# Weight rounding and absolute sums on ScalarE, the feed-forward norms' last operation on GpSimd, and new hand-written orders

## What is computed

```python
x = layernorm(x + attn(x))          # 16 heads of 64, 4 key/value heads, rotary, ALiBi, softmax
x = layernorm(x + xattn(x, ctx))    # 16 heads of 16, windows of 64 and the one before, cell mask, 4 inner norms
x = layernorm(x + ffn(x))           # silu(bitlinear(x, w_gate)) * bitlinear(x, w_up), then w_down
# bitlinear: activations to int8 by row maximum, weights to -1, 0, 1 by the mean of their absolute values
```

## Time and profile before

| | |
|---|---|
| median of 3 runs | 2292.14 us |
| profiled execution | 2293.73 us, of which the span of the instructions is 2291.6 us |
| mean granted TensorE clock | 0.979 |
| PE busy | 2147.3 us (94%) |
| DVE busy | 1954.5 us (85%) |
| ACT busy | 1695.3 us (74%) |
| POOL busy | 1434.2 us (63%) |

### The profile page before, as it was taken

One profiled execution on the slowest core, in us unless ns is written; L12 is line 12 of the kernel. 1 busy time (PEld: TensorE's weight loads), 2 busy tenths in 40 slices (PEclk: granted clock), 3 DMA queues, 4 the chain that ended last, 5 costly groups with the idle time before them and its releaser, 6 DMA issues. The chain is left out here.

```text
span 2291.6 us, 57972 instructions
## 1 busy us (share of the span) xinstructions
PE 2147.3 (94%) x19370; PEld 1649.6 (72%) x19370; DVE 1954.5 (85%) x7981; ACT 1695.3 (74%) x4738; POOL 1434.2 (63%) x1678
## 2 busy tenths in 40 slices
PE   4799999999999999999999999999999999999964
PEld 3577777777777777777777777777777777777742
DVE  5678888889888889988888988888898888889874
ACT  1477777877787887778788777878877778877742
POOL 2466566667766667766666776666677666667531
PEclk8799999999999999999999999999999999999996
DMA  4111100111110001111001111100111110011100
GB/s 133 37 31 27 37 26 23 27 34 36 36 36 24 25 27 33 36 36 36 23 25 28 34 36 36 36 20 23 33 34 36 37 36 14 26 35 35 31 15 10
DMA packets 85397, 74.64 MB, mean 33 GB/s; under 512 B 18544, under 2 KB 79344, under 8 KB 85104
## 3 DMA queue, kind: packets, MB, share of 16 engines
q1 hardware_dynamic: 85104, 70.93, 11.1%
HBM read 45.72 MB, written 8.39 MB: 24 GB/s over the span
## 5 line engine op out<-in xcount | busy, mean ns | idle before, releaser
L1379 POOL TENSOR_TENSOR prob<-prob,precs 128x512 f32<-128x512 f32 x512 | 525.9, 1044 | 218.7 <-DVE precs L1014 216.0
L1287 ACT ACTIVATE prob<-prob,nmax 128x256 f32<-128x256 f32 x1024 | 509.3, 503 | 155.2 <-DVE nmax L1007 155.2
L1007 DVE CUSTOM_DVE_ANT_0 prob<-bank,alibi 128x256 f32<-128x256 f32 x1024 | 371.4, 419 | 13.5 <-PE bank L715 12.4
L611 PE MATMUL bank<-ident,prob 128*128 128x128 f32 x2048 | 315.9, 277 | 5.7 <-ACT pT L1294 5.0
L1311 ACT ACTIVATE px<-px,nmx 128x128 f32<-128x128 f32 x1024 | 315.1, 409 | 4.8 <-DVE nmx L1116 4.8
L1294 ACT COPY pT<-bank 128x512 f32<-128x512 f32 x512 | 300.3, 587 | 12.1 <-PE bank L611 12.0
L611 PEld LDWEIGHTS bank<-ident,prob 128*128 128x128 f32 x2048 | 236.7, 141 | 80.9 <-issue 43.3
L734 PE MATMUL bank<-pT,v_sb 128*64 128x256 f32 x2048 | 250.5, 386 | 5.9 <-DVE qq_lo L998 5.9
L1116 DVE CUSTOM_DVE_ANT_0 px<-bank,mask 128x128 f32<-128x128 f32 x1024 | 225.5, 285 | 29.1 <-PE bank L794 26.2
L623 PE MATMUL bank<-w_hi,x_hi 128*128 128x512 f32 (+1 forms) x512 | 199.2, 389 | 23.6 <-POOL x_lo L1359 16.6
L734 PEld LDWEIGHTS bank<-pT,v_sb 128*64 128x64 f32 x2048 | 142.7, 137 | 101.0 <-issue 45.6
(11 more groups left out here) (211 smaller groups left out, 6104.2 us busy)
## 6 DMA issues: line engine op xcount, KB each, us to landing
raw<-in_xT SPq DMA_DIRECT2D x32, 256.0 KB, 2.9
kx_tok<-in_ctx SPq DMA_DIRECT2D x32, 256.0 KB, 2.9
raw<-in_ctxT SPq DMA_DIRECT2D x32, 256.0 KB, 3.0
xtok<-in_x SPq DMA_DIRECT2D x32, 256.0 KB, 3.0
vs<-vx SPq DMA_DIRECT2D x64, 128.0 KB, 2.9
kx<-k_sin SPq DMA_DIRECT2D x256, 32.0 KB, 2.0
out_y<-x SPq DMA_DIRECT2D x32, 256.0 KB, 2.2
cellk<-in_cell SPq DMA_DIRECT2D x32, 64.0 KB, 3.4
```

What stands on the lines that cost most here:

```text
L611: last = nc.tensor.transpose(bank[:, n * P:(n + 1) * P], src, ident[:])
L1007: v.tensor_tensor_reduce(out=prob[:, (2 * p + q) % SLOTS, c, :], in0=psum[SCORES[c]][:, q * L:(q + 1) * L], in1=alibi[:, p % 2, :], scale= ...
L1287: nc.scalar.activation(prob[:, (2 * p + q) % SLOTS, c, :], prob[:, (2 * p + q) % SLOTS, c, :], ACT.Exp, bias=nmax[:, i:i + 1], scale=-1.0, ...
L1379: g.tensor_tensor(prob[:, n % SLOTS, :, :], prob[:, n % SLOTS, :, :], precs[:, 2 * n:2 * n + 2].unsqueeze(2).to_broadcast([P, 2, L]), ALU. ...
```

## The change

1. High parts of the weights: the copies of `first`, `prep 4` and `wo_split` are taken from DVE and given to ACT. DVE keeps the subtractions and waits for ACT by new semaphores (w_rounded, crossed_rounded).
2. Absolute sums: three DVE reductions become three ACT operations (Abs with an accumulator) that write their unused result over kx. They wait until wo, which lies in kx at first, has been split; kx_clear on POOL now waits for them.
3. SP: of the loads of group 0 only the bias rows still wait for the split of wqkv; wqx, wkvx, wox, ropex and pen go at once. ctx of batch 0 is loaded later, xtok and alibi earlier.
4. X2 and `out` go from ACT to POOL, as (y2 - mean) * rstd with two per-row operands; f_bias and z_bias are gone.
5. BODY, HEAD and TAIL of all five engines are new. On PE both BODYs hold the same 78 matmul steps.

```diff
@@ act
+                    if kind == "first":
+                        i, = args
+                        cols = slice(512 * i, 512 * i + 512)
+                        act.wait_ge(first_loaded[i], 16 * KT)
+                        for k in range(KT):
+                            nc.scalar.copy(w_hi[:, k, cols], raw_w[k][:, cols]).then_inc(w_rounded, 1)
+                    elif kind == "wo_split":
+                        act.wait_ge(later_loaded[1], 16)
+                        nc.scalar.copy(wo_hi[:], raw_wo).then_inc(wo_split, 1)
...
+                        if args[0] == 4:
+                            act.wait_ge(pre_dve, P_CENTRED)
+                            for hi, rawer in ((wkvx_hi, raw_kvx), (wqx_hi, raw_qx), (wox_hi, raw_ox)):
+                                nc.scalar.copy(hi[:], rawer).then_inc(crossed_rounded, 1)
+                        elif args[0] == 5:
+
+                            act.wait_ge(later_loaded[2], 16 * len(later_loads[2]))
+                            act.wait_ge(wo_split, 2)
+                            for m in range(3):
+                                if m > 0:
+                                    act.wait_ge(w_sums, m)
+                                nc.scalar.activation(kx[:].rearrange("p k h n -> p (k h n)"), stage[m], ACT.Abs, accum_out=wsum[:, m:m + 1])\
+                                    .then_inc(w_sums, 1)
...
-                    elif kind == "X2":
-                        act.wait_ge(*landed("stored", b - 1))
-                        act.wait_ge(*at("f_bias", b))
-                        for t in range(TT):
-                            ins = nc.scalar.activation(x2[:, t, :], y2[:, t, :], ACT.Identity, bias=f_bias[:, t:t + 1], scale=f_rstd[:, t:t + 1])
-                        ins.then_inc(sem["x2_ready"], 1)
...
@@ pool
+                    elif kind == "X2":
+                        pool.wait_ge(*landed("stored", b - 1))
                         pool.wait_ge(*at("f_neg", b))
                         pool.wait_ge(*at("f_rstd", b))
-                        g.tensor_tensor(f_bias[:], f_neg[:], f_rstd[:, 0:TT], ALU.mult).then_inc(sem["f_bias"], 1)
+                        pool.sem_inc(waits_passed, 1)
+                        for t in range(TT):
+                            ins = g.tensor_scalar(x2[:, t, :], y2[:, t, :], f_neg[:, t:t + 1], f_rstd[:, t:t + 1], ALU.add, ALU.mult)
+                        ins.then_inc(sem["x2_ready"], 1)
...
@@ BODY["pe"], cut
-        (4, 'HT', 0), (3, 'TX', 1, 1), (3, 'SX', 3), (2, 'T', 13), (3, 'OX', 0), (3, 'TX', 2, 0), (1, 'kT'),
-        (3, 'TX', 2, 1), (4, 'D', 0), (2, 'T', 14), (4, 'HT', 1), (3, 'TX', 3, 0), (1, 'qT', 1), (4, 'D', 1),
...
+        (4, 'HT', 1), (1, 'S', 0), (1, 'qT', 1), (3, 'TX', 3, 0), (4, 'D', 1), (3, 'TX', 3, 1), (2, 'T', 15), (1, 'S', 1),
+        (3, 'OX', 1), (1, 'Q', 0, 2), (3, 'BX', 0), (2, 'O', 3), (1, 'T', 0), (3, 'BX', 1), (1, 'Q', 1, 2), (3, 'NO'),
+        (1, 'T', 1), (1, 'S', 2), (1, 'T', 2), (3, 'PO'), (2, 'W', 1), (2, 'KV', 0), (1, 'V'), (1, 'qT', 2), (1, 'T', 3),
+        (1, 'S', 3), (2, 'KV', 1), (1, 'O', 0), (1, 'T', 4), (2, 'NX'), (0, 'K'), (3, 'XQ'), (1, 'T', 5), (1, 'S', 4),
...
+        (1, 'O', 2), (2, 'TX', 1, 0), (1, 'T', 12), (3, 'HT', 0), (2, 'TX', 1, 1), (2, 'SX', 3), (2, 'OX', 0),
+        (2, 'TX', 2, 0), (1, 'T', 13), (0, 'kT'), (3, 'D', 0), (2, 'TX', 2, 1), (1, 'T', 14),
@@ BODY["pool"], the places of the new steps
+        (2, 'R', 11), (2, 'R', 12), (4, 'HS', 1), (2, 'R', 13), (2, 'R', 14), (2, 'R', 15), (1, 'R', 0), (4, 'ZS'),
+        (1, 'R', 1), (4, 'out'), (1, 'R', 2), (2, 'C'), (1, 'Q', 0, 2), (3, 'OS'), (2, 'CS'), (1, 'Q', 1, 2), (3, 'FS'),
+        (1, 'R', 3), (3, 'X2'), (1, 'R', 4), (3, 'QN'), (1, 'R', 5), (0, 'X'), (1, 'R', 6), (2, 'KV', 1), (1, 'R', 7),
@@ HEAD["pe"], start
-        (0, 'first', 0), (0, 'first', 1), (0, 'V'), (0, 'K'), (0, 'Q', 0, 1), (0, 'Q', 1, 1), (0, 'first', 2),
-        (0, 'prep', 1), (0, 'prep', 2), (0, 'prep', 3), (0, 'qT', 0), (0, 'qT', 1), (0, 'Q', 0, 2), (0, 'Q', 1, 2),
-        (0, 'kT'), (1, 'K'), (0, 'prep', 5), (0, 'KV', 0), (0, 'S', 0), (0, 'S', 1), (0, 'qT', 2), (0, 'T', 0),
...
```

More of the change, by code:

```diff
@@ L115 @@
     "sp": [
-        (0, 'first', 0), (0, 'first', 1), (0, 'first', 2), (0, 'load_xT'), (0, 'tables', 0), (0, 'load_ctx'),
-        (0, 'loads', 0), (0, 'loads', 1), (0, 'load_cell'), (0, 'loads', 2), (1, 'load_xT'), (0, 'load_ctxT'),
-        (2, 'load_xT'), (0, 'load_xtok'), (0, 'tables', 1), (1, 'load_ctxT'), (1, 'load_xtok'), (1, 'load_ctx'),
-        (0, 'load_vs'), (0, 'kx_clear'), (0, 'fill_kx'), (1, 'load_cell'), (3, 'load_xT'), (2, 'load_ctx'),
-        (2, 'load_ctxT'), (2, 'load_xtok'), (2, 'load_cell'), (1, 'fill_kx'), (1, 'load_vs'), (0, 'store'),
-        (3, 'load_cell'), (4, 'load_xT'), (3, 'load_ctx'), (2, 'load_vs'), (2, 'fill_kx'),
+        (0, 'first', 0), (0, 'first', 1), (0, 'first', 2), (0, 'load_xT'), (0, 'tables', 0), (0, 'loads', 0),
+        (0, 'loads', 1), (0, 'load_cell'), (0, 'load_xtok'), (0, 'tables', 1), (0, 'loads', 2), (0, 'load_ctx'),
+        (1, 'load_xT'), (0, 'load_ctxT'), (2, 'load_xT'), (1, 'load_ctxT'), (0, 'kx_clear'), (0, 'fill_kx'),
+        (1, 'load_ctx'), (1, 'load_xtok'), (0, 'load_vs'), (1, 'load_cell'), (2, 'load_cell'), (3, 'load_xT'),
+        (2, 'load_xtok'), (2, 'load_ctxT'), (1, 'load_vs'), (2, 'load_ctx'), (1, 'fill_kx'), (0, 'store'), (4, 'load_xT'),
     ],
     "pe": [
[32 rows of a table removed]
+        (0, 'first', 0), (0, 'first', 1), (0, 'K'), (0, 'Q', 0, 1), (0, 'first', 2), (0, 'prep', 1), (0, 'prep', 2),
[33 rows of a table added]
     ],
@@ L158 @@
         (0, 'first', 0), (0, 'first', 1), (0, 'first', 2), (0, 'prep', 0), (0, 'tables', 0), (0, 'K'), (0, 'Q', 0, 1),
-        (0, 'Q', 1, 1), (0, 'prep', 1), (0, 'prep', 2), (0, 'prep', 3), (0, 'prep', 4), (0, 'qT', 0), (0, 'wo_split'),
[28 rows of a table removed]
+        (0, 'prep', 1), (0, 'prep', 2), (0, 'prep', 3), (0, 'Q', 1, 1), (0, 'prep', 4), (0, 'tables', 1), (0, 'qT', 0),
[30 rows of a table added]
     ],
     "act": [
[26 rows of a table removed]
+        (0, 'first', 0), (0, 'first', 1), (0, 'first', 2), (0, 'X'), (0, 'tables', 0), (0, 'Q', 0, 1), (0, 'Q', 1, 1),
[27 rows of a table added]
     ],
     "pool": [
[15 rows of a table removed]
[15 rows of a table added]
     ],
@@ L555, in run @@
                             sp.dma_start(gb[:].rearrange("p c k -> p (c k)"), a["gb"]).then_inc(gb_loaded, 16)
-                            sp.wait_ge(w_split, 12)
                         elif g == 2:
                             sp.wait_ge(pre_dve, P_CROSSED)
-                        for dst, src in later_loads[g]:
+                        for i, (dst, src) in enumerate(later_loads[g]):
+                            if g == 0 and i == 5:
+                                sp.wait_ge(w_split, 3 * KT)
                             sp.dma_start(dst, src).then_inc(later_loaded[g], 16)
@@ L914, in prepare @@
                         v.tensor_copy(turned_bias[:, m, :, :], psum[5 + m][:].rearrange("p (k n) -> p k n", k=KT)).then_inc(pre_dve, 1)
[L915 to L917 removed]
+                    dve.wait_ge(crossed_rounded, 3)
                     for lo, hi, rawer in ((wkvx_lo, wkvx_hi, raw_kvx), (wqx_lo, wqx_hi, raw_qx), (wox_lo, wox_hi, raw_ox)):
@@ L920, in prepare @@
                     dve.wait_ge(pre_dve, P_CROSSED)
-                elif n == 5:
-                    dve.wait_ge(later_loaded[2], 16 * len(later_loads[2]))
-                    for m in range(3):
-                        v.tensor_reduce(wsum[:, m:m + 1], stage[m], AX_X, ALU.add, apply_absolute_value=True).then_inc(pre_dve, 1)
                 elif n == 6:
@@ L954, in run @@
                         cols = slice(512 * i, 512 * i + 512)
-                        dve.wait_ge(first_loaded[i], 16 * KT)
                         for k in range(KT):
-                            v.tensor_copy(w_hi[:, k, cols], raw_w[k][:, cols]).then_inc(w_split, 1)
-                        for k in range(KT):
-                            dve.wait_ge(w_split, 4 * i + k + 1)
+                            dve.wait_ge(w_rounded, KT * i + k + 1)
                             v.tensor_tensor(w_lo[:, k, cols], raw_w[k][:, cols], w_hi[:, k, cols].bitcast(F32), ALU.subtract).then_inc(w_split, 1)
@@ L963, in run @@
                     elif kind == "wo_split":
-                        dve.wait_ge(later_loaded[1], 16)
-                        v.tensor_copy(wo_hi[:], raw_wo).then_inc(wo_split, 1)
                         dve.wait_ge(wo_split, 1)
@@ L1252, in run @@
                         nc.scalar.copy(c_hi[:], cT[:]).then_inc(sem["c_hi"], 1)
-                    elif kind == "X2":
-                        act.wait_ge(*landed("stored", b - 1))
-                        act.wait_ge(*at("f_bias", b))
-                        for t in range(TT):
-                            ins = nc.scalar.activation(x2[:, t, :], y2[:, t, :], ACT.Identity, bias=f_bias[:, t:t + 1], scale=f_rstd[:, t:t + 1])
```

(12 more changed lines are left out.)

43 lines of the change are left out of this document (21 added, 22 removed), and 365 rows, old and new, of tables (BODY, HEAD, TAIL).

## The result

The changed kernel takes 2279.02 us (median of 6 runs, 2277.73 to 2285.01) against 2292.76 for the kernel before beside it: ratio 0.9943, 95% interval 0.993 to 0.9956. It is 13.7 us faster, where 33 were forecast. The profiled execution took 2278.99 us, its span 2277.0.

What follows compares the result with a forecast made beforehand. PE was taken to bound the kernel, busy 65.66 of 67.08 us a period. Body -20, start-up -13 and drain 0 gave -33 us, from the median 2292.14 to 2259 us; range 2225 to 2288.

Steps and rivals of the forecast that it cites:

- rival C: Body: every joint closed opens another; period stays at 67.08 us, only the start-up pays: 2279 us; chance 0.15.
- PE bounds the body, only its joints can give: Body: PE busy 65.66 of 67.08 us a period; only a shorter path between its steps can help.
- The orders: PE's BODY: 1.4 us of stalls between steps (joints) can go, new neighbours cost 0.65; 0.75 a period, 20 us.
- The upper end: Body's new orders: all joints won, 1.7 us a period, 46 us.
- X2 and `out` on GpSimd: Norm steps moved from ACT to POOL: neither engine becomes the bound, worth nothing by itself; 0 us.
- the R 3 that POOL now runs between FS and X2 is covered: POOL's queue in the body: XQ, which needs QN, moves away from PO, with 16 matmuls between.
- Rival D: POOL's queue: `out` before R 2 delays T 2; +30 us, with 13 from the start-up: 2309 us; chance 0.10.
- The start-up: Before the body: less DVE work, S 0 near 43.5 instead of 73.07; 13 us, ends 5 and 20.
- the copies of `first` on ScalarE: Start of the kernel: six ACT copies of 512 columns, 3.7 us at most; 0 to 0.5 us lost.
- The drain: Chain of the last two batches: loses a handover and a small operation twice; 0 us, from +3 to -4.
- ScalarE's passes: Start-up: a 2048-column pass on ACT takes 1.8 us, between 1.22 and 2.5; Abs would load no table.
- Rival E: Body: GpSimd blocks DVE at the shared port; 30 of 33 us are lost: 2289 us; chance 0.04.

Runs made afterwards that it cites:

- the fastest: Changed kernel with x2 and `out` on ScalarE, `out` behind S 2, and the memsets of kx behind R 7 on GpSimd: 2249.35 us, ratio 0.9811.

## Why the prediction was wrong

The time lay in the range, 20 us over the forecast, and at rival C's 2279. That C's figure fits is luck, since its reason doesn't: not the closed joints but the norm steps took the gain, and its sum leaves out 3 us of the start-up, 2 of the body and the 4 that the drain lost.

- **PE bounds the body, only its joints can give.** Right. Where the period fell clearly, the waits of PE fell with it (marked idle 1.79 us a period in the changed kernel, 1.03 with x2 on ScalarE, 1.11 with `out` there); no engine's busy time became the bound.
- **The orders: 1.4 us of joints less 0.65 given back, 0.75 a period.** The mechanism was right and the term a little small. With both norm steps on ScalarE in good places, the new orders bring 67.08 - 66.05 = 1.03 us a period; how much of it is closed joints and how much new ones take back was not measured apart. The upper end was mis-added: 1.41 us of marked idle times 1.4 is 1.9 or 2.0, not 1.7.
- **X2 and `out` on GpSimd: 0.** This is the step that failed. They cost 66.98 - 66.05 = 0.93 us a period and 2279.0 - 2250.9 = 28 us in all (27 by the ratios), nearly what the orders earn in the body. I argued from the mean: POOL at 46.9 of 67.08 us isn't the bound. But the 7.8 us idle pieces lie elsewhere, and between `out` and QN POOL works without a gap, so much of what is put there comes out at its end: `out`'s 1.09 us made f_var 0.59 us later (0.99 instead of 0.40 behind f_mv). The sentence "the R 3 that POOL now runs between FS and X2 is covered" looked at XQ's distance; the one who waited was DVE's QN, and behind it in DVE's list qT 2, S 3 and KV 1, on which O 0 and NX wait. I named what is queued behind X2 on POOL, and not what is queued behind the reader of x2.
- **Rival D** had the queue right and the victim and the price wrong: PE doesn't wait for T 2, but the `out` that stands ahead of FS by ten operations makes x2 late. A slack could have been read: 1.28 us ahead of f_var in the kernel before. With the old order `out` stays inside it (ratio 1.0001). In the new one nothing of it is left, which only a trace of the new order shows.
- **Rival C** said that a PE that is 97.9% busy opens a joint for each one closed. Three runs with less idle exclude it; the fastest has a period 1.1 us shorter, (2039.5 - 324.2) / 26 = 65.97 by its line of xqT.
- **The start-up: 13 us.** Right, by most of its steps. PE's timeline of the kernel after:

```profile
18.48 4.54 PE L648 MATMUL bank<-pTx,hh 128*128 128x256 f32 x16
26.57 5.41 PE L655 MATMUL bank<-pTx,ones 128*128 128x256 f32 x16 [3.55 <-DVE brow L894]
34.82 1.09 PE L616 MATMUL bank<-ident,px 128*128 128x128 f32 x8 [1.44 <-DVE pTx L914]
...
43.21 0.58 PE L720 MATMUL bank<-kk_hi,qq_hi 64*128 64x256 f32 x2 [1.40 <-DVE kk_lo L988]
```

  Prep 1, 2 and 3 were forecast for 20, 27.5 and 35.7, S 0 for 43.5; DVE's part of S 4, forecast for 80.5, starts at 83.00 instead of 96.83, late by as much as the blocked pass takes beyond its 1.29 us. One small term had the wrong sign: the copies of `first` on ScalarE were to cost 0 to 0.5 us, and PE's first matmul starts at 11.31 instead of 12.45, though that start scatters by nearly 2 us among kernels whose program is the same up to it. The window of the body begins at XQ of batch 2 in both kernels, at 323.7 instead of 340.2: 16.5 us earlier, some 3 more than forecast.
- **The drain: 0, from +3 to -4.** A miss. From XQ of batch 28 to that of batch 31 it went from 178.1 us (2084.2 to 2262.3) to 182.5 (2065.3 to 2247.8): 4.4 us longer. With 16.5 from the start-up and 2.4 from 26 periods (1744.0 - 1741.6) this gives the 14.6 by which the spans differ, within 0.1. In the run with both norm steps on ScalarE in good places the same piece takes 178.9 (2040.56 to 2219.44), so this loss too belongs to x2 and `out` on GpSimd. How the two share it isn't shown: by the line of xqT the piece takes 182.8 us in the changed kernel, 181.6 with x2 alone off POOL, 185.7 with `out` alone off it, and 179.1 with both off it.
- **ScalarE's passes: 1.8 us each, no second table load.** Right. ACT's timeline of the kernel after:

```profile
0.72 1.28 ACT L1343 ACT_TABLE_LOAD   x1 [0.72 <-PEq L1536]
...
36.79 1.90 ACT L1240 CAST wo_hi<-kx 128x2048 fp32r<-128x2048 f32 x1
53.98 1.92 ACT L1256 ACTIVATE kx<-pTx 128x2048 f32<-128x2048 f32 x1
```

  The only table load of the span lies at 0.72 us and lasts 1.28. By the Trainium skill (ScalarE: Activation LUTs, the section on table sets) abs shares a set with exp and tanh; the trace agrees.
- **Rival E, the port.** Not in the body, but in the start-up. L1450, the same operation as in the earlier trace rows, lasts 1115 to 1143 ns in 54 runs, and the new passes of x2 552 to 556. DVE isn't held up there either: over 26 periods it is busy 1552.98 us with x2 and `out` on GpSimd and 1550.63 with both on ScalarE, 0.09 us a period. Where DVE's pass over 2048 columns met POOL in the start-up, one of them stood still, as shown above. The rule of the Trainium skill (SBUF — State Buffer, the section Who interferes with whom) lets a DVE pass in a two-port mode and any GpSimd instruction exclude each other for their whole length; the 3.78 us agree with it if this pass runs in such a mode, which no row tells.
